# A fused decoder layer on one Trainium2 core: two-pass normalization, token mixing moved to VectorE, self stacks loaded in 4 KB rows, and another order of the step

## The chip, the cores and the metric

The kernel runs on 1 core of one Trainium2 chip. The metric is the device time of one execution in microseconds (us), from the start of the program to its end, and lower is better. Engines are called PE (TensorE), PEld (its weight loads), DVE (VectorE), ACT (ScalarE), POOL (GpSimd) and SP (SyncE, which here only issues DMAs).

## What is computed

The reference is one pre-norm decoder layer on x of [64, 128, 128] (batch, tokens, features), in fp32:

```
x = x + self_attention(layernorm(x))            # 16 heads of 8, causal, window 64, softmax over the window
x = x + cross_attention(layernorm(x), ctx, mask) # ctx is [64, 77, 128]; mask adds -100 where it is 1; with biases
x = x + ffn(layernorm(x))
# layernorm(x) = (x - mean) / sqrt(var + 1e-5) over the features, without scale or shift
# ffn(x): x_prev = x one token earlier (zero for the first)
#   xr = mu_r*x + (1-mu_r)*x_prev ; xk = mu_k*x + (1-mu_k)*x_prev
#   out = sigmoid(xr @ W_r.T) * (square(relu(xk @ W_k.T)) @ W_v.T)
```

## The kernel before, in words

**Quads and steps.** The 64 batch entries are worked in 16 quads of 4 (QB = 4, NQ = 16). The kernel is a software pipeline written out by hand: every engine has its own function `step(s)` that is called for s = 0 to 22, and in a step it works on several quads at once; `live(s, k)` guards the piece for quad s-k. Within a step each engine takes its pieces in the listed order, and semaphores join the engines. SP has one queue of its own, in the order that its `step` lists, and a wait on SP holds back every DMA behind it.

**Self attention of a quad.** `stats_x` (DVE, L1389), `moments_x` and `norm_x` (POOL, L934 and L937) normalize x; `turn_x` (PE) transposes it, `project_q/k/v` project it. q and k are split into three bf16 parts each (`high`, `rest`, `mid` and `low_*` on ACT, DVE and POOL), stored to a scratch in HBM (`store_q`, `store_k`, L756 and L752) and loaded back, rearranged, into `qk_stack` (`load_self`, L758 to L772, once for each half u of the heads). `max_upper` and `max_lower` (PE) compute scores for the row maximum, `max_self` (DVE, L1455) reduces them, `turn_max` transposes the maxima, `take_max` and `mid_max` split them, and `load_shift` (SP, L779) puts them as extra rows into `qk_stack`. `scores_upper/lower` (PE) then give shifted scores, `exp_self` (ACT) the exponentials, `attend_*` (PE) the weighted sums; `take_sums`, `turn_sums`, `normalize`, `turn_att`, `project_o` and `add_x1` end it. `qk_stack` has one buffer for each u, so the load of the next quad waits for the last scores of this one.

**Cross attention** goes the same way, with `norm_x1`, `turn_xc`, `project_cq/ck/cv`, `store_cq/ck`, `load_cq` and `load_ck` (SP, L802, into `cq_stack` and `ck_stack`, one buffer for each u), `cross_max` (PE, L478, eight for a quad), `max_cross` (DVE, L1455), `turn_cross_max`, `load_cross_shift` (L816), `cross_scores` (L494), `exp_cross`, `attend_cross` (L509), `turn_cross_sums`, `normalize_cross`, `turn_cross_att`, `project_co` (L528) and `add_x2` (L1508).

**The feed-forward part**: `norm_x2`, `turn_xe`, `take_xeT`, `step_tokens` (POOL, L981: x minus x one token earlier), `mix_k` (DVE, L1517) and `mix_r` (POOL, L990 and L992), `mix_key` and `mix_gate` (PE, L537 and L547), `relu_key`, `square_key`, `tanh_gate`, `mix_value`, `gate_y`, `add_y` (POOL) and `store_y`.

**Buffers that join the pieces.** `score_max` and `score_exp` are one PSUM buffer each: PE may not write the next scores before DVE (max) or ACT (exp) has read the last. `proj[0]` and `proj[1]` are taken in turns by all transposes and projections on PE (`bank`, L280). The profile lists two DMA queues of the kind `instruction`, which bring the program itself to the engines; some 26,600 of its 31,487 instructions are PE's.

**The normalization** is this, for each of the three norms of a quad (n = 0, 1, 2):

```
for b in range(QB):                                                            # L930
    nc.gpsimd.tensor_scalar(xn[n][:, b, :], src[:, b, :], mean[n][:, b:b + 1], root[n][:, b:b + 1],
                            ALU.subtract, ALU.mult).then_inc(ln_out[n], 1)
```

Of the kernel before, what the change touches and what calls it, by code (L numbers as in the profile page):

```python
# [44 lines left out]
def decoder_layer(nc, x, ctx, mask, wq, wk, wv, wo, cwq, cbq, cwk, cbk, cwv, cbv, cwo, cbo,  # L45
# [12 lines left out]
    with ExitStack() as stack:  # L58
# [137 lines left out]
        ln_root = [sem(f"ln_root{n}") for n in range(3)]  # L196
        ln_out = [sem(f"ln_out{n}") for n in range(3)]
# [56 lines left out]
        mix_r_scaled = sem("mix_r_scaled")  # L254
# [20 lines left out]
        def _(pe):  # L275
# [30 lines left out]
            def turn_x(q):  # L306
                pe.wait_ge(ln_out[0], QB * q + QB)
                turn(bank(("xnT", q), (xnT_ready, q + 1)), xn[0], T).then_inc(xnT_made, 1)

            def turn_xc(q):  # L310
                pe.wait_ge(ln_out[1], QB * q + QB)
                turn(bank(("xcT", q), (xcT_ready, q + 1)), xn[1], T).then_inc(xcT_made, 1)

            def turn_xe(q):
                pe.wait_ge(ln_out[2], QB * q + QB)
# [45 lines left out]
            def max_upper(q, u, m):  # L361
                pe.wait_ge(self_in[u], 48 * q + 48)
# [219 lines left out]
            def step(s):  # L582
                if live(s, 2):
                    max_lower(s - 2, 0)
                if live(s, 1):
                    turn_x(s - 1)
                if live(s, 5):
                    cross_scores(s - 5, 0, 0)
                    turn_cross_max(s - 5, 1)
                    attend_cross(s - 5, 0, 2)  # L590
                if live(s, 2):
                    max_upper(s - 2, 0, 1)
                if live(s, 1):
                    project_q(s - 1)
                if live(s, 5):
                    cross_scores(s - 5, 0, 1)
                if live(s, 6):
                    mix_key(s - 6)
                if live(s, 2):
                    max_upper(s - 2, 1, 1)  # L600
                if live(s, 5):
                    attend_cross(s - 5, 0, 1)
                if live(s, 2):
                    turn_max(s - 2, 0)
                if live(s, 1):
                    project_k(s - 1)
                if s == 1:
                    set_up_cross()
                if live(s, 5):
                    attend_cross(s - 5, 0, 0)  # L610
                if live(s, 2):
                    max_lower(s - 2, 1)
                if live(s, 5):
                    cross_scores(s - 5, 1, 3)
                if live(s, 3):
                    turn_sums(s - 3, 1)
                if s == 3:
                    set_up_rest()
                if live(s, 5):
                    turn_cross_sums(s - 5, 0)  # L620
                    cross_scores(s - 5, 1, 2)
                if live(s, 2):
                    max_upper(s - 2, 1, 0)
                if live(s, 5):
                    attend_cross(s - 5, 1, 3)
                if live(s, 3):
                    turn_att(s - 3)
# [1013 lines left out]
```

## Time and profile before

| what | value |
|---|---|
| time, median of 3 runs | 890.24 us (882.71 to 890.93) |
| the profiled execution's own time | 882.54 us |
| its span, first to last instruction | 880.4 us |
| PE busy | 676.6 us (77%), 13293 matmuls and transposes |
| PE weight loads busy | 555.9 us (63%), they overlap the matmuls |
| DVE, ACT, POOL busy | 465.6, 439.7, 456.8 us (53%, 50%, 52%) |
| mean clock granted to PE | 0.842 of full |
| DMA | 93.81 MB, mean 107 GB/s |

Busy times are sums over the instructions of one engine in one execution. A PE matmul's end is modelled, so neighbouring ones overlap in the timeline by some hundredths of a microsecond; the chain of waits shows them without the overlap. The granted clock is 1.0 at 2.4 GHz and 0.5 at 1.2 GHz.

### The profile page before, as it was taken

Reading aid. Unit: us, or ns where it says so; the run is one execution under the profiler, and the core shown is the slowest. Engines: PE = TensorE matmul, PEld = TensorE weight load, DVE = VectorE, ACT = ScalarE, POOL = GpSimd, SP = SyncE. Lnnn points to the kernel's source line nnn. Section 1 sums busy time; section 2 is a strip of 40 time slices with the busy share of each in tenths; the row PEclk is TensorE's granted clock in tenths of the full one; section 3 lists DMA queues with packets and bytes.
Section 4 is the critical chain, followed back from the end, with each engine's and each line's share of the span. In section 5 each row is a group of like instructions: output and inputs, shape, how many; then the busy total and the mean of one; then the engine's idle time right before and its main releaser. Section 6 shows DMA issues by size and latency. Waiting matters only on the chain.

```text
span 880.4 us, 31487 instructions
## 1 busy us (share of the span) xinstructions
PE 676.6 (77%) x13293; PEld 555.9 (63%) x13293; DVE 465.6 (53%) x815; ACT 439.7 (50%) x667; POOL 456.8 (52%) x709
## 2 busy tenths in 40 slices
PE   2357765879778788879688877979898979887683
PEld 2345654667657677668567665868686767665462
DVE  6675353647545456547455454747575656451410
ACT  3042543646546475637455454737574746544230
POOL 7213533255646465755636564565756545644415
PEclk9677887989879799979889798979998989885655
DMA  4753555456545556654656555574757563323000
GB/s 118 98 89 60 104 153 95 139 95 152 96 104 128 108 130 126 140 114 119 96 128 121 106 112 107 139 115 126 129 154 118 133 104 96 101 62 101 10 25 12
DMA packets 86077, 93.81 MB, mean 107 GB/s; under 512 B 16034, under 2 KB 76532, under 8 KB 82868
## 3 DMA queue, kind: packets, MB, share of 16 engines
q1 hardware_dynamic: 85940, 91.81, 49.6%
q8 instruction: 107, 1.75, 1.0%
q14 instruction: 30, 0.25, 0.1%
HBM read 53.32 MB, written 37.40 MB: 103 GB/s over the span
## 4 chain that ended last, share of the span: by engine, by line
PE 44%; DMA 19%; POOL 10%; DVE 8%; issue 8%; SPq 7%; ACT 4%; POOLq 0%; DVEq 0%; ACTq 0%
DMA ck_stack<-ck_scr 14%; PE csums L509 6%; PE proj L302 5%; POOL xn L931 5%; DMA qk_stack<-qk_scr 4%; PE score_exp L494 4%; PE proj L324 4%; SPq L779 4%; PE score_max L368 3%; PE proj L528 3%; PE proj L537 3%; ACT cprobs L1179 2%; PE proj L468 2%; PE sums L433 2%; PE score_max L381 2%
## 5 line engine op out<-in xcount | busy, mean ns | idle before, releaser
L1455 DVE TENSOR_REDUCE cneg_max<-score_max 128x8 f32<-128x616 f32 x128 | 102.0, 797 | 123.4 <-PE score_max L478 123.1
L1179 ACT ACTIVATE cprobs<-score_exp 77x1024 f32<-77x1024 f32 x128 | 129.8, 1014 | 63.3 <-PE score_exp L494 61.7
L931 POOL TENSOR_SCALAR xn<-x,mean,root 128x128 f32<-128x128 f32 x192 | 151.3, 803 | 6.5 <-POOL root L923 6.2
L1455 DVE TENSOR_REDUCE neg_max<-score_max 128x8 f32<-128x1024 f32 (+1 forms) x96 | 117.0, 1219 | 44.2 <-PE score_max L381 27.1
L1179 ACT ACTIVATE probs<-score_exp 128x1024 f32<-128x1024 f32 x96 | 98.0, 1021 | 41.2 <-PE score_exp L399 34.0
L908 POOL TENSOR_TENSOR both<-stats 128x8 f32<-128x8 f32 x48 | 10.2, 212 | 191.1 <-DVE stats L1387 191.1
L478 PE MATMUL score_max<-ck_stack,cq_stack 51*128 51x77 bf16 x1024 | 44.0, 211 | 61.6 <-DMA ck_stack<-ck_scr 58.5
L509 PE MATMUL csums<-cprobs,cv_heads 77*32 77x128 f32 x2048 | 88.2, 303 | 2.5 <-ACT cprobs L1179 2.5
L478 PEld LDWEIGHTS score_max<-ck_stack,cq_stack 51*128 51x128 bf16 x1024 | 27.8, 102 | 76.8 <-DMA ck_stack<-ck_scr 62.6
L302 PE MATMUL proj<-ident,xn 128*128 128x128 f32 x192 | 37.7, 327 | 45.1 <-POOL xn L931 36.7
L494 PE MATMUL score_exp<-cq_stack,ck_stack 53*77 53x128 bf16 x1024 | 60.7, 242 | 11.5 <-ACT cprobs L1179 5.9
L509 PEld LDWEIGHTS csums<-cprobs,cv_heads 77*32 77x32 f32 x2048 | 55.6, 119 | 21.0 <-issue 13.3
L954 POOL TENSOR_TENSOR q_parts<-q_rest,q_parts 128x512 bf16<-128x512 f32 x16 | 18.5, 1156 | 95.5 <-ACT q_parts L1081 95.5
L494 PEld LDWEIGHTS score_exp<-cq_stack,ck_stack 53*77 53x77 bf16 x1024 | 38.8, 124 | 35.0 <-issue 30.1
L368 PE MATMUL score_max<-qk_stack 112*64 112x128 bf16 x1024 | 45.0, 236 | 20.3 <-DMA qk_stack<-qk_scr 14.2
L302 PEld LDWEIGHTS proj<-ident,xn 128*128 128x128 f32 x192 | 26.7, 169 | 48.6 <-POOL xn L931 28.2
L368 PEld LDWEIGHTS score_max<-qk_stack 112*64 112x64 bf16 x1024 | 34.1, 118 | 30.0 <-issue 17.5
L923 POOL TENSOR_TENSOR root<-var,neg_half 128x4 f32<-128x4 f32 x48 | 50.3, 1048 | 3.8
L399 PE MATMUL score_exp<-qk_stack 114*128 114x64 bf16 x1024 | 47.1, 205 | 6.1 <-ACT probs L1179 5.6
L399 PEld LDWEIGHTS score_exp<-qk_stack 114*128 114x128 bf16 x1024 | 42.7, 106 | 9.5 <-issue 6.6
L433 PE MATMUL sums<-probs,v_heads 128*32 128x64 f32 x2048 | 44.9, 242 | 1.9 <-issue 1.9
L324 PE MATMUL proj<-xnT,wT 128*128 128x128 f32 x256 | 42.7, 320 | 2.2 <-DVE q_rest L1404 1.3
(142 smaller groups left out, 1435.9 us busy)
## 6 DMA issues: line engine op xcount, KB each, us to landing
qk_stack<-qk_scr SPq DMA_DIRECT2D x32, 384.0 KB
cq_stack<-cq_scr SPq DMA_DIRECT2D x64, 192.0 KB, 4.1
qk_stack<-qk_scr SPq DMA_DIRECT2D x32, 256.0 KB
ck_stack<-ck_scr SPq DMA_DIRECT2D x64, 122.7 KB
qk_scr<-q_parts SPq DMA_DIRECT2D x16, 384.0 KB, 2.8
qk_scr<-k_parts SPq DMA_DIRECT2D x16, 384.0 KB, 2.9
cq_scr<-cq_parts SPq DMA_DIRECT2D x16, 384.0 KB, 3.4
x<-in_x_dram SPq DMA_DIRECT2D x16, 256.0 KB, 3.3
```

Of the source, the lines that this page charges most:

```text
L302: last = nc.tensor.transpose(dst[:, rows * b:rows * b + rows], src[0:rows, b, :], ident[0:rows, 0:rows])
L324: last = nc.tensor.matmul(dst[:, n * b:n * b + n], wT[:, w, :], src[:, n * b:n * b + n], start=True, stop=True)
L368: last = nc.tensor.matmul(score_max[HALF * j:HALF * j + HALF, c:c + T], qk_stack[0:ROW1, u, 0, j, i, 2 * m + b, HALF:T], qk_stack[0:ROW1, ...
L399: last = nc.tensor.matmul(score_exp[:, c:c + HALF], qk_stack[0:ROWS_SELF, u, 1, j, i, 2 * m + b, :], qk_stack[0:ROWS_SELF, u, 0, j, i, 2 * ...
L433: last = nc.tensor.matmul(sums[32 * i:32 * i + 32, 2 * m + b, HALF:T], v_heads[:, 2 * m + b, H // 2 * u + 2 * i + j, :], probs[:, m, c:c + ...
L478: last = nc.tensor.matmul(score_max[:, c:c + TC], cq_stack[r:r + ROWS_BIAS, u, i, b, :], ck_stack[r:r + ROWS_BIAS, u, i, b, :], start=True ...
L494: last = nc.tensor.matmul(score_exp[0:TC, c:c + T], ck_stack[r:r + ROWS_CROSS, u, i, b, :], cq_stack[r:r + ROWS_CROSS, u, i, b, :], start= ...
L509: last = nc.tensor.matmul(csums[32 * i:32 * i + 32, b, :], cv_heads[0:TC, b, H // 2 * u + 2 * i + j, :], cprobs[0:TC, b, c:c + T], start=( ...
L923: nc.gpsimd.tensor_tensor(root[n][:, :], var4[n][:, :], neg_half[:, :], ALU.pow).then_inc(ln_root[n], 1)
L931: nc.gpsimd.tensor_scalar(xn[n][:, b, :], src[:, b, :], mean[n][:, b:b + 1], root[n][:, b:b + 1], ALU.subtract, ALU.mult).then_inc(ln_out[ ...
L1179: nc.scalar.activation(dst, src, ACT.Exp).then_inc(exp_done, 1)
L1455: nc.vector.tensor_reduce(dst, src, AX_X, ALU.max, negate=True).then_inc(max_taken, 1)
```

## The change

It has four parts. (1) The norm takes two instructions over the whole quad in place of four over one batch entry each. (2) `mix_r` goes from two POOL instructions to one on DVE. (3) `load_self` issues six DMAs with rows of 4 KB where it issued three with rows of 8 KB; the bytes are the same. (4) Every engine's `step` lists its pieces in another order. A few waits change with it.

```
-                pe.wait_ge(ln_out[0], QB * q + QB)          # the same for ln_out[1] and ln_out[2]
+                pe.wait_ge(ln_out[0], q + 1)
...
-                pe.wait_ge(self_in[u], 48 * q + 48)         # the same in copy_k_low on DVE
+                pe.wait_ge(self_in[u], 96 * q + 96)
...
                 for (c, n, first_q), (_, _, first_k) in zip(RUNS_Q, RUNS_K):
-                    src = bass.AP(tensor=flat.tensor, offset=flat.offset + first_q * DH * row + u * UT,
-                                  ap=[[row, DH * n], [(3 + first_k - first_q) * DH * row, 2], [1, UT]])
                     r = ROW0 + DH * c
-                    sp.dma_start(qk_stack[r:r + DH * n, u].rearrange("r t j i b s -> r t (j i b s)"), src)\
-                        .then_inc(self_in[u], 16)
+                    for j in range(J):
+                        src = bass.AP(tensor=flat.tensor, offset=flat.offset + first_q * DH * row + (J * u + j) * UT // J,
+                                      ap=[[row, DH * n], [(3 + first_k - first_q) * DH * row, 2], [1, UT // J]])
+                        sp.dma_start(qk_stack[r:r + DH * n, u, :, j].rearrange("r t i b s -> r t (i b s)"), src)\
+                            .then_inc(self_in[u], 16)
...
             def norm_of(n, src, turned, q):
                 if q:
                     pool.wait_ge(turned, q)
+                pool.wait_ge(ln_moments[n], 6 * q + 6)
+                nc.gpsimd.tensor_tensor(xn[n][:, :, :], src[:, :, :],
+                                        mean[n][:, :].unsqueeze(2).to_broadcast([P, QB, D]), ALU.subtract)\
+                    .then_inc(ln_centred[n], 1)
                 pool.wait_ge(ln_root[n], q + 1)
-                for b in range(QB):
-                    nc.gpsimd.tensor_scalar(xn[n][:, b, :], src[:, b, :], mean[n][:, b:b + 1], root[n][:, b:b + 1],
-                                            ALU.subtract, ALU.mult).then_inc(ln_out[n], 1)
+                pool.wait_ge(ln_centred[n], q + 1)
+                nc.gpsimd.tensor_tensor(xn[n][:, :, :], xn[n][:, :, :],
+                                        root[n][:, :].unsqueeze(2).to_broadcast([P, QB, D]), ALU.mult)\
+                    .then_inc(ln_out[n], 1)
...
             def add_bias(q):
-                pool.wait_ge(ln_out[1], QB * q + QB)
+                pool.wait_ge(ln_centred[1], q + 1)
...
             def step_tokens(q):
                 if q:
                     pool.wait_ge(mix_k_ready, q)
+                    pool.wait_ge(mix_r_ready, q)
...
-            def mix_r(q):
-                if q:
-                    pool.wait_ge(fr_made, q)
-                else:
-                    pool.wait_ge(small_in, 64)
-                pool.wait_ge(step_ready, q + 1)
-                nc.gpsimd.tensor_scalar(mixed[:, 0], x_step[:, :, :], mu[:, 0:1], None, ALU.mult).then_inc(mix_r_scaled, 1)
-                pool.wait_ge(mix_r_scaled, q + 1)
-                nc.gpsimd.tensor_tensor(mixed[:, 0], mixed[:, 0], xeT[:, :, 0:T], ALU.add).then_inc(mix_r_ready, 1)
...
             def add_y(q):
-                pool.wait_ge(ln_out[2], QB * q + QB)
+                pool.wait_ge(ln_centred[2], q + 1)
...
             def divide(src, turned, inv, inv_ready, dst, dst_turned, ready, q, u):
+                if 2 * q + u:
+                    dve.wait_ge(ready, 2 * q + u)
...
+            def mix(q, m, multiplied, ready):
+                if q:
+                    dve.wait_ge(multiplied, q)
+                else:
+                    dve.wait_ge(small_in, 64)
                 dve.wait_ge(step_ready, q + 1)
+                nc.vector.scalar_tensor_tensor(out=mixed[:, m], in0=x_step[:, :, :], scalar=mu[:, m:m + 1],
+                                               in1=xeT[:, :, 0:T], op0=ALU.mult, op1=ALU.add).then_inc(ready, 1)
+
+            def mix_k(q):
+                mix(q, 1, fk_made, mix_k_ready)
+
+            def mix_r(q):
+                mix(q, 0, fr_made, mix_r_ready)
```

At the program's start the loads of `wo`, the three ffn weights and the small vectors come ahead of x of quads 1 and 2, and `set_up_rest` and `set_up_out_bias` run in step 1, where they ran in step 3.

The new order of a step, engine by engine: the first number is k, so that the piece works on quad s-k, and behind the semicolon stand its other arguments (u, or u and m or b).

```
PE:   attend_cross(6;1,2) project_cq(4) turn_max(3;1) scores_upper(3;0,0) cross_max(5;0,3)
      attend_cross(6;1,0) attend_cross(6;1,3) attend_cross(6;1,1) cross_max(5;0,1) scores_upper(3;0,1)
      turn_cross_sums(6;1) turn_ctx(4) cross_max(5;0,2) scores_lower(3;0) project_cv(5) cross_max(5;0,0)
      attend_upper(3;0,1) attend_lower(3;0) turn_cross_att(6) cross_max(5;1,2) turn_cross_max(5;0)
      scores_upper(3;1,1) project_co(6) cross_max(5;1,0) scores_lower(3;1) attend_upper(3;0,0)
      cross_max(5;1,3) project_ck(4) scores_upper(3;1,0) turn_sums(3;0) cross_max(5;1,1) attend_lower(3;1)
      attend_upper(3;1,1) attend_upper(3;1,0) project_v(2) turn_cross_max(5;1) cross_scores(5;0,2)
      turn_x(1) turn_sums(3;1) max_upper(2;0,1) project_q(1) project_k(1) max_lower(2;0)
      cross_scores(5;0,0) attend_cross(5;0,2) turn_att(3) max_upper(2;0,0) cross_scores(5;0,1) turn_xe(6)
      project_o(3) cross_scores(5;0,3) attend_cross(5;0,1) turn_max(2;0) max_upper(2;1,0)
      cross_scores(5;1,3) attend_cross(5;0,3) attend_cross(5;0,0) mix_key(6) cross_scores(5;1,0)
      mix_gate(6) max_upper(2;1,1) cross_scores(5;1,2) mix_value(6) turn_cross_sums(5;0) max_lower(2;1)
      turn_xc(3) cross_scores(5;1,1)
SP:   load_ctx(3) store_y(7) load_self(2;0) load_cross_shift(5;0) store_cq(4) load_self(2;1)
      load_cross_shift(5;1) store_ck(4) load_x(0) load_cq(4;0) load_shift(2;0) load_ck(4;0) store_q(1)
      store_k(1) load_cq(4;1) load_ck(4;1) load_shift(2;1)
POOL: add_y(7) add_bias(6) norm_x(1) low_cq(4) moments_x2(6) norm_x2(6) low_ck(4) low_q(1)
      step_tokens(6) moments_x1(3) square_key(6) norm_x1(3) low_k(1) moments_x(0)
DVE:  max_cross(5;0,3) mid_max(3;1) rest_cq(4) max_cross(5;0,1) normalize_cross(6;1) max_cross(5;0,2)
      max_cross(5;0,0) max_cross(5;1,2) mid_cross_max(5;0) max_cross(5;1,0) add_x2(6) max_cross(5;1,3)
      stats_x2(6) rest_ck(4) max_cross(5;1,1) normalize(3;0) spread_v(2) mid_cross_max(5;1)
      copy_k_low(2;0) normalize(3;1) max_self(2;0,1) rest_q(1) max_self(2;0,2) rest_k(1) max_self(2;0,0)
      add_x1(3) stats_x1(3) mix_k(6) mid_max(2;0) mix_r(6) max_self(2;1,0) copy_k_low(2;1)
      max_self(2;1,1) gate_y(6) normalize_cross(5;0) max_self(2;1,2) stats_x(0)
ACT:  take_xcT(4) exp_cross(6;1,1) high_cq(4) take_max(3;1) exp_self(3;0,0) take_cross_sums(6;1)
      exp_self(3;0,1) mid_cq(4) exp_self(3;0,2) take_ctxT(4) spread_cv(5) take_cattT(6)
      take_cross_max(5;0) exp_self(3;1,1) exp_self(3;1,2) take_sums(3;0) high_ck(4) exp_self(3;1,0)
      mid_ck(4) take_sums(3;1) take_cross_max(5;1) take_xnT(1) exp_cross(5;0,2) high_q(1) high_k(1)
      mid_q(1) exp_cross(5;0,0) take_attT(3) exp_cross(5;0,1) take_xeT(6) exp_cross(5;0,3)
      take_max(2;0) spread_v_low(2) exp_cross(5;1,3) relu_key(6) exp_cross(5;1,0) tanh_gate(6)
      take_cross_sums(5;0) mid_k(1) exp_cross(5;1,2)
```

## Rows read from the trace of the kernel before

**Rows 1.** Windows; after each length: PE, PEld, DVE, ACT, POOL busy, clock, DMA share, GB/s.
```profile
156.00:680.00 524.00, 437.35 (x9118) 363.21 (x9116) 294.52 (x538) 295.70 (x450) 299.56 (x468) 0.89 0.58 120
...
595.00:636.00 41.00, 36.87 (x827) 30.93 (x822) 25.60 (x50) 26.74 (x41) 26.62 (x43) 0.96 0.61 120
```
**Rows 2.** Timeline of ACT: the copies of the transposed x of quads 3 and 15.
```profile
108.14 0.60 ACT L1123 ACTIVATE xnT<-proj 128x512 f32<-128x512 f32 x1 [0.83 <-PE proj L302]
...
679.82 0.60 ACT L1123 ACTIVATE xnT<-proj 128x512 f32<-128x512 f32 x1 [0.61 <-PE proj L302]
```
**Rows 3.** Waits of PE from 156 to 680: total us, times, longest us.
```profile
PE score_max L478 <- DMA ck_stack<-ck_scr: 44.8, 11, 5.8
PE proj L302 <- issue: 8.3, 2, 4.2
PE proj L302 <- POOL xn L931: 7.2, 8, 1.3
...
PE score_max L381 <- issue: 3.0, 1, 3.0
```
**Rows 4.** Timeline of PE: an idle stretch of 6.57 us put down to issue.
```profile
542.36 0.27 PE L448 MATMUL sums<-probs,v_low 128*32 128x64 f32 x1 [6.57 <-issue]
```
**Rows 5.** DMA queues: the larger one that carries instructions; packets, MB, share of 16 engines.
```profile
q8 instruction: 107, 1.75, 1.0%
```
**Rows 6.** Timeline of PE: `turn_max(s-2, 1)`, and the wait for `ck_stack` behind it.
```profile
609.64 0.27 PE L389 MATMUL proj<-ident,neg_max 128*32 128x128 f32 x1
...
620.96 0.32 PE L478 MATMUL score_max<-ck_stack,cq_stack 51*128 51x77 bf16 x8 [2.56 <-DMA ck_stack<-ck_scr]
```
**Rows 7.** Timeline of SP in the same step.
```profile
611.60 1.22 SPq L779 DMA_DIRECT2D qk_stack<-max_mid  x2
612.92 0.76 SPq L802 DMA_DIRECT2D ck_stack<-ck_scr  x2
```
**Rows 8.** The chain of waits: start, us, what (here the DMAs to landing).
```profile
104.66 9.54 DMA qk_stack<-qk_scr
...
366.41 9.32 DMA ck_stack<-ck_scr
...
743.06 5.15 DMA ck_stack<-ck_scr
```
**Rows 9.** The chain of waits between 540 and 592: what one piece takes on PE.
```profile
549.43 0.57 PE score_max L368 x16
550.00 1.09 PE proj L324 x8
551.09 0.35 PE score_exp L494 x8
...
553.09 0.57 PE csums L509 x16
...
555.35 0.62 PE score_max L381 x32
...
559.15 0.59 PE proj L302 x4
```
**Rows 10.** Timeline of PE: `project_co`, and `turn_xe` behind it.
```profile
623.75 1.86 PE L528 MATMUL proj<-wT,cattT 128*128 128x128 f32 x8
...
634.47 0.66 PE L302 MATMUL proj<-ident,xn 128*128 128x128 f32 x4 [1.33 <-POOL xn L931]
```
**Rows 11.** Groups by line: count, busy us, mean ns, idle before.
```profile
L931 POOL TENSOR_SCALAR xn<-x,mean,root 128x128 f32<-128x128 f32 x192 | 151.3, 803 | 6.5 <-POOL root L923 6.2
L990 POOL TENSOR_SCALAR mixed<-x_step,mu 128x512 f32<-128x512 f32 x16 | 27.4, 1714 | 0.2 <-POOL x_step L981 0.2
...
L973 POOL TENSOR_TENSOR x<-x,out_bias 128x512 f32<-128x512 f32 x16 | 20.3, 1267 | 0.0
L992 POOL TENSOR_TENSOR mixed<-mixed,xeT 128x512 f32<-128x512 f32 x16 | 19.2, 1198 | 1.3
...
L1517 DVE SCALAR_TENSOR_TENSOR mixed<-x_step,mu,xeT 128x512 f32<-128x512 f32 x16 | 18.2, 1138 | 10.3 <-POOL x_step L981 10.3
```

More of the change, by code:

```diff
@@ L582, in step @@
             def step(s):
+                if live(s, 6):
+                    attend_cross(s - 6, 1, 2)
+                if live(s, 4):
+                    project_cq(s - 4)
+                if live(s, 3):
+                    turn_max(s - 3, 1)
+                    scores_upper(s - 3, 0, 0)
+                if live(s, 5):
+                    cross_max(s - 5, 0, 3)
+                if live(s, 6):
+                    attend_cross(s - 6, 1, 0)
+                    attend_cross(s - 6, 1, 3)
+                    attend_cross(s - 6, 1, 1)
@@ L594, in step @@
                     project_q(s - 1)
+                    project_k(s - 1)
+                if s == 1:
+                    set_up_cross()
+                    set_up_rest()
+                if live(s, 2):
+                    max_lower(s - 2, 0)
+                if live(s, 5):
+                    cross_scores(s - 5, 0, 0)
+                    attend_cross(s - 5, 0, 2)
+                if live(s, 3):
+                    turn_att(s - 3)
+                if live(s, 2):
+                    max_upper(s - 2, 0, 0)
                 if live(s, 5):
@@ L597, in step @@
                 if live(s, 6):
+                    turn_xe(s - 6)
+                if live(s, 3):
+                    project_o(s - 3)
+                if live(s, 5):
+                    cross_scores(s - 5, 0, 3)
+                    attend_cross(s - 5, 0, 1)
+                if live(s, 2):
+                    turn_max(s - 2, 0)
+                    max_upper(s - 2, 1, 0)
+                if live(s, 5):
+                    cross_scores(s - 5, 1, 3)
+                    attend_cross(s - 5, 0, 3)
+                    attend_cross(s - 5, 0, 0)
+                if live(s, 6):
                     mix_key(s - 6)
+                if live(s, 5):
+                    cross_scores(s - 5, 1, 0)
+                if live(s, 6):
+                    mix_gate(s - 6)
                 if live(s, 2):
@@ L601, in step @@
                 if live(s, 5):
[L602 to L608, printed above, removed]
+                    cross_scores(s - 5, 1, 2)
+                if live(s, 6):
+                    mix_value(s - 6)
                 if live(s, 5):
-                    attend_cross(s - 5, 0, 0)
+                    turn_cross_sums(s - 5, 0)
```

526 lines of the change are left out of this document (236 added, 290 removed).

## Prediction

> **What bounds the kernel now.** I read the windows first. In the long middle stretch PE is busy 437 of 524 us while DVE, ACT and POOL are each busy under 300 [rows 1]: PE is the engine that sets the pace, and no other comes near. Next I took the length of a step. The copies of the transposed x of quads 3 and 15 start at 108.1 and 679.8 us, so 12 steps take 571.7 us, 47.6 us each [rows 2]; one more of the same kind follows before the pipeline drains, so 13 steps of 47.5 us (617 us) are what the change can act on. What lies ahead and behind (265 us) is fill and drain.
>
> How short could a step be? The middle stretch of 524 us has 9118 matmuls, 829 in each of its 524 / 47.5 = 11 steps; the stretch of 41.0 us has 827, so it holds one step, and there PE is busy 36.9 us at a granted clock of 0.96. I take 37.0 us as a step's work [rows 1]. The reader is to see that the usual step is 10 us longer than that. The middle stretch tells where they are:
>
> - PE waits for the load of `ck_stack` for 44.8 us, 11 times, so once in every step: 4.1 us [rows 3].
> - PE waits for `xn`, the norm, for 7.2 us: 0.65 a step [rows 3].
> - PE stands idle with nothing released late ("issue"): six entries of the waits, 8.3 us the largest and 3.0 the smallest shown, 29.6 in all, 2.7 us a step [rows 3]. A single one took 6.57 us [rows 4], in the middle of a run of equal matmuls. I read this as PE out of instructions: they come by DMA, 107 packets with 1.75 MB [rows 5], which share the DMA engines with the loads.
> - The clock: PE busy is 437.35 / 11 = 39.7 us a step at 0.89 against 37.0 at 0.96 [rows 1]: 2.7 us.
> - The rest, 47.5 - 37.0 - 4.1 - 0.65 - 2.7 - 2.7 = 0.4 us.
>
> **The change, part by part**
>
> *Two-pass norm.* Removed: four instructions of 803 ns, 3.21 us a norm [rows 11]. Added: two over the whole quad. No row shows them. From below they cost what L992 does, 1.20 us each, from above L973's 1.27, a row with a broadcast operand like theirs [rows 11]; I take 2.54 us, so 0.67 us less for each of three norms. The second waits for the first by a semaphore on its own engine; the pair L990, L992, which does the same, idled 1.3 us in 16 times, under 0.1 us each. POOL is no bound, so this counts only where PE waits for a norm (below).
>
> *mix_r on DVE.* POOL loses 1.71 + 1.20 = 2.91 us a quad, DVE gains one instruction as L1517, mean 1.14 us [rows 11]. DVE's total goes from 294.5 / 11 = 26.8 to 27.9 us a step. It stands, however, where DVE is dense: from `add_x1` to `stats_x` the new order puts some 11 us of DVE work beside some 11 us of PE work, and three of PE's `max` pieces wait for DVE there. Below nothing it can't go; above, all of it and a second wait, 2 us. I take 0.5 us a step.
> Beside this, POOL and DVE share a way into SBUF, by the Trainium skill, "SBUF — State Buffer", whose glossary calls it an exclusive lock where the loser fully blocks. The group's own mean already holds such blocking if it is there; the sum stays as it is.
>
> *Order: the wait for ck_stack.* In the step shown, `turn_max(s-2,1)` is at 609.64, the shift DMAs behind it end their issue at 612.82, `ck_stack` is issued at 612.92 and PE resumes at 620.96, 2.56 us late [rows 6, 7]. So the load is issued 3.3 us behind that transpose and takes 8 us, while PE has only 8.8 us of other work. The load took 9.32 us in another step, and 5.15 us at 743 us, when no self load was left in the program [rows 8]. Now the new order. `load_ck(s-4,0)` stands behind `load_shift(s-2,0)`, which waits for `turn_max(s-2,0)` and for `mid_max`, which DVE reaches after `add_x1`, `stats_x1` and `mix_k`: I reckon 4 us from transpose to issue. Its user is `cross_max(s-5,0,3)` of the next step. Between them PE has, by the pieces of [rows 9]: 2 `max_upper` (1.14), 4 `cross_scores` (1.40), 3 `attend_cross` (1.71), 4 projections (4.36), 2 turns (1.18), `max_lower` (0.62), `turn_max` and `scores_upper` (0.8 by the same rows): 11.2 us. No self load is issued within it; those come a quarter and a half into the next step. So the data are there 4 + 5.15 = 9.2 to 4 + 9.32 = 13.3 us behind the transpose, the stall is 0 to 2.1 us, and the row without a self load beside it is the nearer one: I take 0.5 us. The load for u=1 is issued at the start of the next step and used 10 us into it, so it is covered as well. From 4.1 to 0.5.
>
> *Order: the wait for xn.* From `project_co` at 623.75 to `turn_xe` at 634.47 are 10.7 us, with 1.33 of idle, so the chain through `add_x2`, statistics, moments and norm takes that long [rows 10]. In the new order PE has about 14 us of work between the two, and the chain is 0.67 us shorter. `turn_x` has its norm 10 us early. `turn_xc` is tight: 9 us behind `project_o`, with `square_key` put ahead of the norm on POOL. I take 0.1 us a step: 0.65 goes to 0.1.
>
> *Six self transfers.* The bytes are the same. A load took 9.54 us [rows 8]. SP issues three DMAs more for each u, some 0.35 us each. The new order has 13.3 us of PE work between the last scores of u=0 and the first `max_upper` of the next quad, and 13.9 us for u=1; less 2.1 us for six issues, 11 us are left for a landing. From below I take half of 9.54 (shorter rows that go through faster), from above 9.54 plus 5.15, as if the second half came as a short load of its own behind the first: 14.7. At 9.54 nothing is late: 0 us. What may change is the starving of PE's instructions, which share the DMA engines with these rows. Bounds: all 2.7 us stay, or all go (and, since PE runs its program in less time, up to 1 us more may come). I take 2.0 us.
> The Trainium skill says two things on this, both in "DMA: Bandwidth & Descriptors". In "Queues, rings and completion order" each DMA engine takes turns between queues at packet granularity, and a later table gives a packet as preferably at most 4096 B; by that, 4 KB rows would let the instruction fetch in sooner, and the term would be near 0, the whole 2 us better. Against the change speaks "Bandwidth": a fixed cost near 2 us a DMA and its rule to batch. No row decides between them; the second is a rival below, priced from rows.
>
> *Clock.* With fewer and shorter stalls the clock stays up more: in the step with 4.1 us of idle it was 0.96, on average 0.89 [rows 1]. Of the 2.7 us I leave 1.6 (bounds 0 and 2.7).
>
> *Added waits.* `divide` waits for its own earlier write on DVE, `step_tokens` on POOL for `mix_r` of the quad before, done a step ago: both are met when they are reached, so nothing queued behind them (the norm of x1 on POOL, the maxima on DVE) is held: 0. `add_bias` and `add_y` now wait for the first pass only, which frees nothing that PE waits for. On SP, `load_self` is moved behind the second shift load of the quad before and `load_ck` behind the first of its own; both are in the reckoning above.
>
> *Fill, drain, start-up.* Seen in real time each piece keeps its distance from x's load: the new step boundary is moved by about half a step, not the depth. I take 0 (bounds: 10 us either way, for the different order in which the few live pieces meet, and `set_up_rest` in step 1).
>
> **Sum.** A step: 37.0 + 0.5 (ck) + 0.1 (xn) + 2.0 (issue) + 1.6 (clock) + 0.5 (DVE) + 0.4 (rest) = 42.1 us, 5.4 less than 47.5. Over 13 steps 70 us. The profiled execution took 882.5 us (span 880.4 and 2.1 around it), so 812.5. The median of the runs, 890.2, is 7.7 above that execution; random starving is my guess for this spread, and less of it is left, so I add a third: **815 us**. A measurement can tell some 1% here.
>
> **The rivals**
>
> 1. *The waits change places* (0.13). The ck load takes 9.32 us anyway because stores and `cq_stack` run beside it (stall 2.1), starving and clock stay at 2.7 each. Step 37.0 + 2.1 + 0.1 + 2.7 + 2.7 + 0.5 + 0.4 = 45.5, 26 us off the median: 864 us. For it: neither starving nor clock follows from the order alone. Against: the 5.15 us row.
> 2. *No gain* (0.08). As rival 1, and the tight places (DVE in the second half, `turn_xc`, the shift rows queued behind the self loads) cost 2 us more: step 47.5, 890 us.
> 3. *Slower: six transfers make the self load the last to arrive* (0.12). Place: `max_upper(s-2,0,1)` and `max_upper(s-2,1,0)`, L368, "waits for DMA qk_stack". It costs PE 2 x (L - 11) us a step for a landing of L. From L = 13.7 us on it eats the 5.4 us and the kernel is slower. At the upper bound, 14.7, the step is 42.1 + 7.4 = 49.5, with the fill's loads later as well: 915 us. For it: there is one buffer for each u, so the load can't be issued earlier, and a transfer more is a completion more. Against: equal bytes, 11 us of cover, and 9.54 us measured. A fixed 2 us for each of three more DMAs, as the skill's page has it, would give 15.5 us if they came one after another.
> 4. *Other slower outcomes* (0.03), such as more starving because two self loads follow each other closely.
>
> That 4 KB rows don't do what they are for leaves the forecast: it has only 0.7 us a step from it.
>
> **Chances.** Forecast 0.64, with 784 to 845 as its own range (step 39.8 to 44.5). Faster by over 1%: forecast and rival 1, 0.77. Same: 0.08. Slower: 0.15. The range for 8 in 10 goes from 784 to 878, which takes in rival 1 and leaves out rival 3 and most of rival 2.
>
> **What would show it.** In the profile after: xnT copies 42 us apart; PE busy over 85% of the middle windows with a clock of 0.93 or more; the wait of L478 for `ck_stack` under 10 us in all; "L302 waits for POOL xn" nearly gone; the norm as two groups of 1.27 us; L368 without a wait for `qk_stack` in the middle; "issue" near 2 us a step, or far under it if the shorter rows help. Wrong would be: steps over 46 us; a wait of over 3 us a step on one line, at L368 (rival 3) or L478 (rival 1); or a drain longer by over 10 us.

## The result, and the profile after

The changed kernel takes 810.3 us (median of 4 runs, 801.2 to 815.5) against 886.5 us (4 runs, 881.4 to 890.9); the ratio is 0.907, with a 95% interval of 0.895 to 0.918. A second timing on another chip gave 805.6 us and 0.900 (0.892 to 0.909). The forecast was 815 us, in a range of 784 to 878, with 0.77 on faster. The profiled execution took 814.7 us, a slow one among its runs; the base was a quick one among its own, so the two profiles differ by less (68 us) than the medians do (76 us).

The head of the page of the changed kernel, with its DMA queues:

```profile
span 812.9 us, 31580 instructions
...
PE 663.0 (82%) x13293; PEld 546.6 (67%) x13293; DVE 478.4 (59%) x831; ACT 434.2 (53%) x667; POOL 375.3 (46%) x581
...
q1 hardware_dynamic: 90164, 91.81, 51.4%
q8 instruction: 107, 1.75, 1.0%
```

PE's share rises from 77 to 82%, POOL's busy time falls from 457 to 375 us, and the bytes are the same 91.81 MB.

The timeline of ACT has the copies of the transposed x of quads 3 and 15, the answer to [rows 2], and the window between them answers to [rows 1]:

```profile
116.94 0.60 ACT L1115 ACTIVATE xnT<-proj 128x512 f32<-128x512 f32 x1 [0.91 <-PE proj L302]
...
625.31 0.60 ACT L1115 ACTIVATE xnT<-proj 128x512 f32<-128x512 f32 x1 [1.22 <-PE proj L302]
```

```profile
116.94:625.31 508.37, 453.95 (x9703) 376.67 (x9704) 326.25 (x587) 306.75 (x475) 262.52 (x404) 0.92 0.62 136
```

So 12 steps take 508.4 us, 42.4 us each, where it was 47.6. PE is busy 37.8 us of a step and idle 4.5. The first two of the twelve are not full yet (601 and 804 matmuls). In the ten full ones behind them (205.50 to 625.31 us, 830 matmuls each) a step is 42.0 us with PE busy 38.1 at a clock of 0.96, and before (202.42 to 679.82 us) it was 47.7 us with PE busy 40.0 at 0.89. Thirteen steps less by 5.3 us are 69 us, all of the 68 us between the profiles; ahead of and behind the steps nothing changed in sum (880.4 - 13 x 47.6 = 262 before, 812.9 - 13 x 42.4 = 262 after).

PE's waits in this stretch (total us, times, longest us), the answer to [rows 3]:

```profile
PE score_max L368 <- issue: 7.2, 3, 3.8
PE sums L433 <- issue: 6.0, 3, 2.8
PE proj L302 <- DVE v_heads L1427: 4.6, 10, 0.5
PE score_exp L399 <- DMA qk_stack<-max_mid: 3.5, 4, 1.7
...
PE score_exp L494 <- DMA cq_stack<-cmax_mid: 3.2, 3, 1.5
PE proj L330 <- POOL k_act L990: 3.2, 7, 0.5
...
PE score_max L478 <- DMA ck_stack<-ck_scr: 0.9, 1, 0.9
...
PE proj L302 <- POOL xn L931: 0.5, 1, 0.5
```

The reader is to see what is gone and what stays: the wait for `ck_stack` fell from once a step, 4.1 us, to 0.9 us in all, that for `xn` to 0.5, and nothing took their place but small entries. The idle put down to issue stays: its entries sum to 28.6 us, 2.4 us a step.

The timelines of PE and SP around one ck load, the answer to [rows 6] and [rows 7]:

```profile
339.09 0.29 PE L389 MATMUL proj<-ident,neg_max 128*32 128x128 f32 x1
...
350.55 0.32 PE L478 MATMUL score_max<-ck_stack,cq_stack 51*128 51x77 bf16 x8
```

```profile
341.62 1.22 SPq L776 DMA_DIRECT2D qk_stack<-max_mid  x2
342.94 0.74 SPq L799 DMA_DIRECT2D ck_stack<-ck_scr  x2
...
355.51 2.31 SPq L768 DMA_DIRECT2D qk_stack<-qk_scr  x6
```

From the transpose of the maxima to the issue are 3.9 us (reckoned: 4), from the transpose to the first use 11.5 (reckoned: 11.2), and the use has no idle before it: the load landed in under 7.6 us, with no self load until it was done.

The costs by group, beside [rows 11]:

```profile
L931 POOL TENSOR_TENSOR xn<-xn,root 128x512 f32<-128x512 f32 x48 | 50.2, 1045 | 7.5 <-POOL xn L926 0.9
L926 POOL TENSOR_TENSOR xn<-x,mean 128x512 f32<-128x512 f32 x48 | 49.8, 1038 | 0.0
...
L1508 DVE SCALAR_TENSOR_TENSOR mixed<-x_step,mu,xeT 128x512 f32<-128x512 f32 x32 | 23.2, 736 | 21.9 <-POOL x_step L983 21.9
```

A norm's two passes take 2.08 us, not 2.54, and each mixing on DVE 0.74 us, not 1.14.

### The profile page after: what moved, and what is told of

Same layout as the page of the kernel before. It is cut to its first block, busy times and chain, and to the rows that moved or that the text cites. A ratio compares the mean times of both kernels' runs of the same rounds, so it can differ in the third digit from the quotient of the medians.

```text
span 812.9 us, 31580 instructions
## 1 busy us (share of the span) xinstructions
PE 663.0 (82%) x13293; PEld 546.6 (67%) x13293; DVE 478.4 (59%) x831; ACT 434.2 (53%) x667; POOL 375.3 (46%) x581
## 3 DMA queue, kind: packets, MB, share of 16 engines
q1 hardware_dynamic: 90164, 91.81, 51.4%
q8 instruction: 107, 1.75, 1.0%
## 4 chain that ended last, share of the span: by engine, by line
PE 61%; issue 9%; POOL 8%; DVE 8%; DMA 6%; ACT 5%; SPq 1%; POOLq 0%; ACTq 0%; DVEq 0%
PE proj L302 9%; PE proj L324 7%; PE csums L509 6%; PE proj L330 6%; PE score_exp L399 4%; PE score_exp L494 4%; PE sums L433 4%; PE score_max L368 3%; ACT probs L1171 3%; PE score_max L478 3%; DMA qk_stack<-max_mid 3%; DMA cq_stack<-cmax_mid 3%; PE score_exp L412 3%; PE score_max L381 3%; PE sums L448 2%
## 5 line engine op out<-in xcount | busy, mean ns | idle before, releaser
L1444 DVE TENSOR_REDUCE neg_max<-score_max 128x8 f32<-128x1024 f32 x96 | 117.1, 1220 | 56.4 <-PE score_max L368 45.5
L904 POOL TENSOR_TENSOR both<-stats 128x8 f32<-128x8 f32 x48 | 15.6, 324 | 181.6 <-DVE stats L1376 181.6
L509 PE MATMUL csums<-cprobs,cv_heads 77*32 77x128 f32 x2048 | 79.8, 293 | 2.1 <-issue 2.1
L302 PE MATMUL proj<-ident,xn 128*128 128x128 f32 x192 | 36.2, 319 | 36.5 <-POOL xn L931 32.4
L368 PE MATMUL score_max<-qk_stack 112*64 112x128 bf16 x1024 | 46.8, 240 | 18.7 <-issue 10.5
L919 POOL TENSOR_TENSOR root<-var,neg_half 128x4 f32<-128x4 f32 x48 | 57.0, 1187 | 3.8
L368 PEld LDWEIGHTS score_max<-qk_stack 112*64 112x64 bf16 x1024 | 35.1, 120 | 29.6 <-issue 25.8
L399 PEld LDWEIGHTS score_exp<-qk_stack 114*128 114x128 bf16 x1024 | 42.6, 105 | 16.8 <-issue 10.2
L931 POOL TENSOR_TENSOR xn<-xn,root 128x512 f32<-128x512 f32 x48 | 50.2, 1045 | 7.5 <-POOL xn L926 0.9
L302 PEld LDWEIGHTS proj<-ident,xn 128*128 128x128 f32 x192 | 23.6, 158 | 41.3 <-POOL xn L931 23.6
L478 PE MATMUL score_max<-ck_stack,cq_stack 51*128 51x77 bf16 x1024 | 42.1, 203 | 10.6 <-DVE cneg_max L1444 4.8
L433 PE MATMUL sums<-probs,v_heads 128*32 128x64 f32 x2048 | 43.1, 232 | 8.9 <-issue 8.9
L926 POOL TENSOR_TENSOR xn<-x,mean 128x512 f32<-128x512 f32 x48 | 49.8, 1038 | 0.0
L478 PEld LDWEIGHTS score_max<-ck_stack,cq_stack 51*128 51x128 bf16 x1024 | 24.8, 98 | 29.3 <-issue 21.9
```

Source lines behind the costliest of these rows:

```text
L302: last = nc.tensor.transpose(dst[:, rows * b:rows * b + rows], src[0:rows, b, :], ident[0:rows, 0:rows])
L368: last = nc.tensor.matmul(score_max[HALF * j:HALF * j + HALF, c:c + T], qk_stack[0:ROW1, u, 0, j, i, 2 * m + b, HALF:T], qk_stack[0:ROW1, ...
L399: last = nc.tensor.matmul(score_exp[:, c:c + HALF], qk_stack[0:ROWS_SELF, u, 1, j, i, 2 * m + b, :], qk_stack[0:ROWS_SELF, u, 0, j, i, 2 * ...
L433: last = nc.tensor.matmul(sums[32 * i:32 * i + 32, 2 * m + b, HALF:T], v_heads[:, 2 * m + b, H // 2 * u + 2 * i + j, :], probs[:, m, c:c + ...
L478: last = nc.tensor.matmul(score_max[:, c:c + TC], cq_stack[r:r + ROWS_BIAS, u, i, b, :], ck_stack[r:r + ROWS_BIAS, u, i, b, :], start=True ...
L509: last = nc.tensor.matmul(csums[32 * i:32 * i + 32, b, :], cv_heads[0:TC, b, H // 2 * u + 2 * i + j, :], cprobs[0:TC, b, c:c + T], start=( ...
```

## The experiments

Two theories stood against each other. Theory A, the prediction's: the order brings the gain, by the ck load and the norms; the row split and the rest bring a few microseconds. Theory B: the changed self load frees the DMA engines and so feeds everything else. Each run was timed against the kernel before on the same chip. "A step" is again from quad 3's xnT copy to quad 15's, over 12; "issue" is the sum of PE's issue entries between them, for a step.

| run | median us | ratio to before | step us | issue us a step |
|---|---|---|---|---|
| e1, the changed kernel | 805.6 | 0.900 (0.892 to 0.909) | 42.6 | 2.3 |
| e2, it with three transfers, 8 KB | 824.8 | 0.925 (0.917 to 0.934) | 42.8 | 3.5 |
| e3, it with the four-pass norm | 819.9 | 0.919 (0.912 to 0.925) | 43.0 | 2.7 |
| e4, it with mix_r on POOL | 838.0 | 0.933 (0.924 to 0.942) | 43.6 | 3.0 |
| e5, before with six transfers | 874.1 | 0.966 (0.951 to 0.981) | 46.3 | 1.2 |
| e6, before with all but the order | 868.9 | 0.965 (0.954 to 0.977) | 45.9 | 2.2 |
| e7, before with ck_stack first | 852.4 | 0.945 (0.932 to 0.958) | 45.2 | 4.0 |
| e8, changed, three transfers again | 827.7 | 0.919 (0.907 to 0.931) | 42.9 | 3.1 |
| e9, e6 and e7 together | 832.3 | 0.934 (of medians) | 43.7 | 2.1 |
| e10, changed, twelve of 2 KB rows | 778.5 | 0.874 (of medians) | 40.2 | 1.7 |
| e11, changed, ck load as 48 + 3 rows | 802.5 | 0.901 (of medians) | 41.7 | 2.8 |
| e12, changed, twelve of 4 KB rows | 775.2 | 0.872 (0.865 to 0.879) | 39.3 | 1.1 |

The last two columns come from one profiled execution each, and single executions of one kernel differ by 1 to 2%, so a step or an issue sum that differs by a few tenths tells nothing; where a verdict hangs on medians, they decide. Where the ratio is one of medians, no interval is on record; the kernel before has its median within 890 to 895 us on all four chips of the experiments.

**The parts taken out of the changed kernel, one by one.** e1 is the base.

> The changed kernel itself, as the base for its variants on the same chip. Expected: a ratio of 0.907 to the kernel before (0.895 to 0.918), about 805 us, 42.4 us between the xnT copies, as in its first timing. Both theories say the same here.

e2 undoes the row split:

```
+                    src = bass.AP(tensor=flat.tensor, offset=flat.offset + first_q * DH * row + u * UT,
+                                  ap=[[row, DH * n], [(3 + first_k - first_q) * DH * row, 2], [1, UT]])
                     r = ROW0 + DH * c
-                    for j in range(J):
...
+                    sp.dma_start(qk_stack[r:r + DH * n, u].rearrange("r t j i b s -> r t (j i b s)"), src)\
+                        .then_inc(self_in[u], 16)
```

> The changed kernel, with the self load back at three transfers with rows of 8 KB. Theory A (the new order brings the gain; the rows bring at most the starving of PE's instructions): 0 to 9 us slower than the changed kernel (ratio to before 0.907 to 0.918), with the same waits on ck_stack, and about 0.7 us a step more idle put down to issue. Theory B (the shorter rows free the DMA engines, and with them come the earlier ck_stack and the fed PE): over 25 us slower (ratio over 0.935), ck_stack waited for again by over 2 us a step.

It came out between the two: 19 us slower than e1, twice what theory A allowed, but with no wait for `ck_stack` at all, which theory B wanted. What grew is the idle put down to issue. In e2's timeline of PE, and then in the changed kernel's, the same stall, in front of the last 10 of the same 32 matmuls of L433:

```profile
451.36 0.59 PE L433 MATMUL sums<-probs,v_heads 128*32 128x64 f32 x10 [6.13 <-issue]
```

```profile
448.26 0.38 PE L433 MATMUL sums<-probs,v_heads 128*32 128x64 f32 x10 [1.93 <-issue]
```

The stall sits at a place in the program, inside a run of matmuls that wait for nothing, and only its length differs. The traces can say more. With weight loads, matmuls and semaphore waits counted in order of start, PE runs 27,584 instructions, and the queue q8 brings 1.75 MB in 107 packets: 16 KB each, one for every 256 instructions. In the fourteen traces of this case there are 198 places where PE stands still for over 1 us in front of an instruction that waits for no semaphore. All 198 fall on the same instruction of a block of 256, and each ends 1.2 to 2.3 us after one of those packets has landed. So these stalls are PE out of instructions, and that reading of [rows 4] is shown. The Trainium skill, "Runtime: NRT & Kernel Launch", section "Instruction fetch mechanics", describes a sequential prefetch in blocks of 16 KiB, 256 instructions, that are brought by DMA, which agrees with this spacing. It also says that the fetch is hidden, since instructions are issued more slowly than they are brought; here stalls of up to 6.6 us show that it is not always.

What delays the packet is seen in part. In the four traces with rows of 8 KB (the kernel before, e2, e7, e8) the self load's packets can be told by their size. When PE entered the block ahead of such a stall, one of them was under way in 39 of 68 cases; when it entered one that no stall followed, in 106 of 356. A self load under way makes a stall likelier, but it is not the only thing that does.

e3 puts the norm back to four instructions (and the counts of `ln_out` with it):

```
-                nc.gpsimd.tensor_tensor(xn[n][:, :, :], src[:, :, :],
...
-                nc.gpsimd.tensor_tensor(xn[n][:, :, :], xn[n][:, :, :],
...
+                for b in range(QB):
+                    nc.gpsimd.tensor_scalar(xn[n][:, b, :], src[:, b, :], mean[n][:, b:b + 1], root[n][:, b:b + 1],
+                                            ALU.subtract, ALU.mult).then_inc(ln_out[n], 1)
```

> The changed kernel, with the norm back at four instructions of 803 ns in place of two of 1041 ns, so POOL has 1.1 us more for each norm, 3.4 us a step. Theory A (the norms are covered, but turn_xc is tight, 0.1 us of slack by the reckoning): PE waits up to 1.1 us a step for xn at turn_xc, 0 to 14 us slower (ratio to before up to 0.922). Rival (the cheaper norm is what the new order lives on): PE waits at turn_xc and then at its followers, over 20 us slower.

14 us slower, at the edge of theory A's 0 to 14, and by its mechanism. Of PE's waits of e3 in the stretch, this is the one for the norm, in front of `turn_xc` each time:

```profile
PE proj L302 <- POOL xn L927: 10.9, 11, 1.8
```

That is 0.9 us a step, against 0.5 us in all the twelve with two passes: the tight place is real.

e4 puts `mix_r` back on POOL behind `step_tokens`, as the two instructions of the kernel before (the first hunk is POOL's step, the second DVE's):

```
                 if live(s, 6):
                     step_tokens(s - 6)
+                    mix_r(s - 6)
...
-                if live(s, 6):
-                    mix_r(s - 6)
```

> The changed kernel, with mix_r back on POOL as two instructions, right behind step_tokens. It adds 2.9 us to POOL just ahead of the moments and the norm of x1, which turn_xc awaits with no slack, and takes 1.14 us from DVE where it is dense. Theory A: moments_x1 starts about 2.4 us later, but square_key, which the norm follows, waits for relu anyway until some 4 us behind it, so turn_xc is late by 0 to 1.5 us: 0 to 20 us slower. Rival (moving work to DVE costs more than it gives): 5 us or more faster than the changed kernel.

32 us slower, beyond theory A's 20, and the place was another. PE's waits of e4:

```profile
PE proj L331 <- POOL k_act L1000: 16.6, 10, 1.8
```

It is `mix_value` that waits, for `square_key`, which stands on POOL behind the moments and is pushed back by them; `turn_xc` appears once, with 0.2 us. That wait makes up 1.4 us a step less the changed kernel's 0.3, 13.4 us over the twelve steps. The profiled execution of e4 took 828.3 us, 13.6 more than that of the changed kernel, so the wait covers the difference of these two; why the medians lie 32 us apart isn't seen in it and stays open. e4 tests one place for `mix_r` on POOL; another might cost less.

**The parts put into the kernel before.** e5 has the split of the load alone, e6 all parts but the order (two-pass norm, `mix_r` on DVE behind `mix_k`, six transfers).

> The kernel before, with the self load alone changed to six transfers with rows of 4 KB. Theory A: within 1% (870 to 890 us): ck_stack stays late by 3 to 4 us a step, since its issue time is set by the shift load ahead of it; issue idle 2.7 us a step or up to 1 us less. Theory B (rows free the DMA engines): 25 us or more faster, ck_stack's landing falls from 9 towards 6 us. Rival 3 of the prediction (six transfers land later): slower, with L368 waiting for qk_stack in the middle stretch.

> The kernel before in its old order, with the three other parts of the change: two-pass norm, mix_r on DVE right behind mix_k, six transfers. Theory A: 0 to 12 us faster than before (the 0.65 us a step of xn goes, ck_stack's wait stays), so the order is worth over 60 us of the 76. Rival: 30 us or more faster, so the parts carry much of the gain.

e5 is 21 us faster where theory A said within 1%. Its four executions lie far apart (856.5 to 888.4 us), so the size is uncertain, though the interval of 0.951 to 0.981 does not reach 1. Its waits show where not:

```profile
PE score_max L478 <- DMA ck_stack<-ck_scr: 58.5, 12, 7.8
```

The ck wait is as large as before (52.6 us between the same quads), so theory B's path, an earlier landing, is not taken. What fell is the issue sum, from 32.7 to 13.8 us. And e6 is no better than e5: in the old order the norm and `mix_r` bring nothing that these runs can tell, though in the new one they are worth 14 and 32 us. The faster norm did its part in e6 too (PE's wait for `xn` is 0.2 us in all, against 7.2 before), but the wait for `ck_stack` stayed at 50.8 us; that it took up what the norm gave is my reading, and no run shows it.

e7 is the kernel before with two pieces of SP exchanged:

```
                 if live(s, 4):
                     load_cq(s - 4, 1)
-                if live(s, 2):
-                    load_shift(s - 2, 1)
                 if live(s, 4):
                     load_ck(s - 4, 1)
+                if live(s, 2):
+                    load_shift(s - 2, 1)
```

> The kernel before, with only load_ck(s-4,1) moved ahead of load_shift(s-2,1) on SP, so that ck_stack is issued some 3.3 us earlier than behind that shift load. If the wait for ck_stack is a cost by itself (4.1 us a step, 53 us in 13 steps), 3.3 us of it goes and the kernel is 30 to 45 us faster. If it only hides something else that is as late (the starved PE, the next wait), it is under 12 us faster although L478's wait is nearly gone.

42 us faster, within the 30 to 45 expected if the wait is a cost by itself. The wait for `ck_stack` is gone from its list, and the next in line has come up:

```profile
PE score_exp L399 <- DMA qk_stack<-max_mid: 19.1, 10, 8.7
...
PE score_max L368 <- DMA qk_stack<-qk_scr: 5.9, 4, 2.7
```

The 4.1 us a step became 1.6 for the shift rows, now behind the ck load, and the issue sum is larger (47.8 us against 32.7). e9 joins e6 and e7, to see whether the parts add.

> The kernel before in its old order with the three other parts (as in the run with all but the order, ratio 0.965) and load_ck(s-4,1) ahead of load_shift(s-2,1) (alone 0.945). Theory A (the parts act on different terms, starving and ck_stack, and add): 0.965 x 0.945 = 0.912, so all but some 0.01 of the new order's worth is this one wait. Rival (the other 1,500 moves of the new order matter by themselves, or the waits behind ck_stack, for the shift rows and for instructions, take their place): 0.93 or more, with L399 waiting for max_mid by 1.5 us a step.

They don't add to 0.912: it is 0.934, the rival's side, and the shift rows take more than half of what `ck_stack` gave (50.8 us in e6, gone in e9):

```profile
PE score_exp L399 <- DMA qk_stack<-max_mid: 30.8, 11, 8.4
```

So the one exchange gives more than half of the whole gain, and moving one load alone moves the wait. The last 0.03 come from the rest of the new order. In it both loads have room, and the two waits that e9 is left with (30.8 us for the shift rows, 4.6 for the self load) are 3.5 and 0.6 us; which of its many moves does this was not tried one by one.

**The self load: rows or transfers.** e8 was to have three transfers with rows of 4 KB, by an address pattern that names the halves apart:

```
+                    src = bass.AP(tensor=flat.tensor, offset=flat.offset + first_q * DH * row + u * UT,
+                                  ap=[[row, DH * n], [(3 + first_k - first_q) * DH * row, 2], [UT // J, J], [1, UT // J]])
```

> The changed kernel, with three transfers for each u whose rows are still 4 KB (the address pattern names the halves apart). It tells the number of transfers from the length of rows. If only the row length matters, it is as the changed kernel; if the three DMAs more cost something on SP or in landings, it is 2 to 8 us faster; if the pattern is put together to 8 KB rows again (no packet of 4 KB from this load), it is as the run with three transfers of 8 KB.

The page of e8 and that of e2 have the same counts of packets, here e8's line, so the halves were put together and its rows were 8 KB again:

```profile
DMA packets 86078, 93.81 MB, mean 114 GB/s; under 512 B 16034, under 2 KB 76532, under 8 KB 82868
```

It repeats e2 on another chip (0.919 and 0.925) and says nothing of the row length. e10 splits each half once more, so that there are twelve transfers with rows of 2 KB:

```
                     for j in range(J):
+                        for h in range(2):
...
+                            sp.dma_start(qk_stack[r:r + DH * n, u, :, j, 2 * h:2 * h + 2]
+                                         .rearrange("r t i b s -> r t (i b s)"), src).then_inc(self_in[u], 16)
```

> The changed kernel, with the self load in twelve transfers with rows of 2 KB for each u. If what starves PE is how long a row holds a DMA engine, issue idle falls again (from 2.4 us a step to under 1.5) and, unless SP's six issues more (2.1 us a load) come late, the kernel is 0 to 15 us faster than the changed one (0.90). If 4 KB was the point beyond which shorter rows give nothing (as a packet of 4096 B in the Trainium skill, DMA: Bandwidth & Descriptors, would have it), issue idle stays near 2.4 us and the kernel is the same or up to 10 us slower.

27 to 32 us faster than the changed kernel in its two timings, twice the most I expected. e10 changes the rows and the number of transfers together, though. e12 keeps rows of 4 KB and makes twelve transfers by loading the rows of q and of k apart:

```
                     for j in range(J):
+                        for t in range(2):
...
+                            sp.dma_start(qk_stack[r:r + DH * n, u, t, j].rearrange("r i b s -> r (i b s)"), src)\
+                                .then_inc(self_in[u], 16)
```

> The changed kernel, with twelve transfers for each u as in the run with 2 KB rows, but with rows of 4 KB (q and k rows apart). It tells the row length from the number of transfers, which also spreads the load over the 4 to 6 us that SP takes to issue it. If the row length keeps PE fed, it is as the changed kernel (ratio to before 0.90, issue idle 2.4 us a step) or a little slower. If the spreading does it, it is as the run with 2 KB rows (ratio 0.874, issue idle 1.7 us a step).

e12 is as fast as e10 or a little faster, and beats both kernels of the case: 0.872 of the kernel before, some 30 us under the changed one. So what twelve transfers give, their number gives, or the smaller size of each, and not the row length: 2 and 4 KB come out the same. For the step from three to six the two are not told apart, since e8 did not get its rows of 4 KB. What twelve do is seen in SP's timeline of e12: one u takes 5.84 us to issue, where six took 2.31, and the bytes come to the DMA engines spread out.

```profile
369.99 5.84 SPq L770 DMA_DIRECT2D qk_stack<-qk_scr  x12
```

And the head of e12's page has the DMA engines' time for the same bytes:

```profile
span 768.5 us, 31772 instructions
...
q1 hardware_dynamic: 92468, 91.82, 49.9%
```

49.9% of 768.5 us is 383 us of 16 engines, against 49.6% of 880.4, 437 us, before the change and 51.4% of 812.9, 418 us, after it. e2, with three transfers in the new order, has 415, so six are no better in this than three; with twelve a packet of 4 KB takes 0.33 us in the mean, with six 0.38. e10 has 50.6% of 783.2, 396 us. The sum of issue falls from 2.4 to 1.1 us a step and the clock of the middle rises from 0.92 to 0.97. In the ten full steps of e12 (191.84 to 585.12 us) a step is 39.3 us and PE is busy 36.5 of it at a clock of 1.00. The changed kernel had 42.0 and 38.1 at 0.96, so of the 2.7 us saved 1.6 are the same matmuls run at the higher clock. That the spreading in time does this, and not something else that goes with twelve transfers (which rows share an engine), was not tried.

**e11: the load of ck_stack.** Its 51 rows were split into 48 and 3:

```
                 for j in range(J):
+                    for r0, r1 in ((0, NROWS), (NROWS, rows))[:1 + (rows > NROWS)]:
...
-                pe.wait_ge(ck_in[u], 32 * q + 32)
+                pe.wait_ge(ck_in[u], 64 * q + 64)
```

> The changed kernel, with each load of ck_stack (51 rows) split in two transfers, 48 rows and 3 rows. The 51 rows run on few DMA engines, the 48 like cq_stack's, whose load lands in some 4 us. The wait for ck_stack is gone already, so by theory A the middle stays the same (within 0.5%) and the drain, where L478 waits for ck_stack once, gains under 2 us. If these long runs of rows on few engines are what keeps instructions from PE, issue idle falls by 1 us a step or more and the kernel is over 10 us faster.

802.5 us and 0.901: the same as the changed kernel (0.907 and 0.900), issue 2.8 us a step. With the wait gone, a quicker load is worth nothing, and these rows are not what starves PE. The Trainium skill, "DMA: Bandwidth & Descriptors", section "Why a DMA increments its semaphore by 16 and not by 1", has a rule for the number of DMA engines by which 51 rows run on 3 and 48 on 16; no row shown here counts engines, and the time doesn't depend on it.

## Why the prediction was right

The time (815 against 810), the step (42.1 against 42.4) and the place of the gain held, though not the worth of each part: that the terms below add up so well is in part luck. Term by term, for a step of the changed profile:

- **ck_stack**, 4.1 to 0.5: right, 0.1 measured. The gate (4 us), the cover (11.2 us) and the choice of the row without a self load beside it held. e7 shows that moving this load alone is worth 5.5%, with a part of the wait handed on to the shift rows.
- **xn**, 0.65 to 0.1: right, 0.04. e3 confirms the tight `turn_xc`.
- **Work**, 37.0, and **clock**, 1.6: right in kind, a little too much in size. The 37.8 us of the twelve steps count some that aren't full. In the ten full ones PE was busy 38.1 us where it was 40.0, so the clock left 1.1 over my 37.0. That figure held some of the clock itself, since it was read at 0.96: at 1.00 the same matmuls take 36.5 (e12). I expected a clock of 0.93 or more in the middle windows; it is 0.92 over the twelve steps and 0.96 over the ten.
- **Issue**, 2.0: 2.4 in the profile, and right in size, but the step on the six transfers failed beneath it. I gave the split 0.7 us a step, 9 us in all. Undoing it costs 19 us (e2), adding it alone to the kernel before gives 21 (e5). The size was off by a factor of two. That these loads keep instructions from PE is borne out by the traces. That shorter rows are the reason is not: at twelve transfers their length makes no difference (e10, e12), and at three it was never tried alone. The rest of the sum holds without it: 815 + 9 = 824 us is 0.926 of 890, and the changed kernel with three transfers measured 0.925 (e2) and 0.919 (e8). So the 5 to 10 us by which the forecast was too slow are about what the split was undervalued by. The third of 7.7 us that I added for the spread of the runs had no support: the median after lies 4 us below the profiled execution, not above it.
- **DVE**, 0.5, and the rest, 0.4: no wait over 0.4 us a step stands on one line. What is left of the 4.5 us of idle, 2.0 us, is spread over a dozen small waits, the shift rows' 0.6 the largest. The 0.5 is also the term with the wrong sign. I put `mix_r` on DVE down as a cost of up to 6.5 us in the whole. Its instruction takes 0.74 us, not 1.14, and putting it back on POOL in the new order costs 32 us (e4). I had counted POOL as no bound, and left out that `mix_value` waits for `square_key`, which stands behind it there; that wait is 13.4 us of the 32, and the rest stays open.
- **Fill and drain**, 0: right, 262 us both times.

Rival 1 (the waits change places) is what e7 and e9 do, and the changed kernel does not. Rival 3 (six transfers land too late) is wrong by its mechanism: L368 waited for `qk_stack` 0.6 us in the whole stretch, and twelve transfers, with a longer issue still, 0.5. The fixed cost of about 2 us for each DMA stands in the Trainium skill, "DMA: Bandwidth & Descriptors", under "Anatomy of one DMA — SWDGE (gpsimd) path", and not in "Bandwidth", which has the rule to batch; it was measured there for DMAs that GpSimd issues, and SP issues these. It may hold for one landing; here, where no one waits for the load's end, more and smaller transfers won. The other rule, turns at packets of up to 4096 B, could be behind some of the 19 us between three and six transfers, which no run separates; it does not explain the 30 us more of e12, whose rows are 4 KB as well.

## What to carry to other kernels

When a load is late on an in-order DMA queue, measure from the event that gates the piece ahead of it, and compare that with the work the consumer has in between; exchanging two entries of the queue was worth 5.5%, but it made the next entry late, so both have to be given room. Where PE's profile shows idle put down to issue at fixed places of the program, look whether the places lie whole multiples of 256 instructions apart, and then at large loads that are issued in a burst: cutting one that nobody waits for into more transfers cost SP some microseconds and gave 4% on an already improved kernel. Take a part out of the new version as well as putting it into the old: the norm and the mixing looked worthless in the old order and were worth 2 and 4% in the new one.

## What the runs showed that I had not expected

- The same 91.8 MB cost the 16 DMA engines 437 us before, 415 to 421 in the new order with three or six transfers (the changed kernel, e1 to e4, e8), and 383 and 396 with twelve. So the same bytes don't always cost the same; that it is how loads lie against each other was not tried.
- An address pattern with contiguous halves named apart gives the same packets as one without (86078, of which 82868 under 8 KB, in e8 as in e2).
- A mixing on DVE takes 728 to 752 ns in the changed kernel, 32 times; before it took 729 to 1669. The instruction is the same, and what runs beside it on POOL is not; that POOL is the cause was not tried.
